# Reordering TensorE across units, spreading VectorE's other work over the weight steps, and a new DRAM layout for unit vectors and values

## The chip, the core and the metric

One core of one Trainium2 chip runs the whole program. The metric is the device time of one execution, in microseconds (us).

## The reference

The input `x` is [8, 32, 128, 128]. Two blocks follow each other, each on a group-normalized copy:

```python
x = x + wavelet_conv(gn(x), w0, w1, w2, bias)   # 3 Haar levels, a 5x5 conv of 128 channels on each
x = x + local_similarity(gn(x), spatial)
# local_similarity, K = 5:
dot    = einsum('bchw,bckhw->bkhw', x, patches)          # patches: the 25 shifted copies
sim    = dot / maximum(norm_x * norm_p, 1e-8)
weight = (sim + 1) * 0.5 * spatial_weight
out    = einsum('bckhw,bkhw->bchw', patches, weight)
```

## The kernel before

There are eight images. Iteration `i` of the main loop does the wavelet convolution of image `i` and the local similarity of image `b = i - 1`, interleaved. Iteration 0 has the convolution alone, iterations 1 to 7 have both, iteration 8 the similarity alone.

An iteration has a head and eight units. In the head the second normalization is found, the low-pass bands are made, levels 2 and 1 are convolved (L1232), and the unit vectors of units 0 and 1 are prepared. The level-0 convolution has eight points of 30 matmuls each (`conv_points`, L1258); each point is worked on together with one unit (half a band of the image) of the local similarity, so "unit j" is both.

What TensorE does beside the 30 matmuls is placed by `hook`, at the nine places `HOOKS`, k = 0 to 8. In each of the steps k = 0 to 7 `gram` (L1320) makes the products of keys and queries in one of two PSUM banks; `key_values` (L1303) turns the values around in two parts (before: k = 0 and k = 4), and `filter_group` (L1342) multiplies values by weights (before: k = 3, 5, 7 and 8). `norm_piece` (L1281) and `count_short` (L1291) prepare unit j + 2.

VectorE turns each product bank into weights (`weights`, L980), eight times in a unit. `gram` of step k waits until the weights of step k - 2 are made, and the weights of step k wait for `gram` of step k. Between the weights VectorE does all its other work by a list written out by hand in `iteration`: `units_open`, `units_refine`, `units_close`, `value_lows` and `unit_lows` (L948) of unit j + 2, `result` (L994) of unit j - 1, and the convolution's inputs and sums (`wino_in`, `wino_low`, `sums`, `accumulate`, `finals`, `add_up`, `image_stats`). The statistics of the next image (`raw_stats`, L741) stand in the head: four before `wino_delta`, two after the first unit vectors, two after `level1_out`.

Unit vectors and values go through DRAM. When `unit_lows` of unit h is done, the SyncE queue (SP) runs `save_half`: three transfers, `d_hl` (L374), `d_v` (L375) and `d_n` (L376). Then `load_unit` waits until all of them have landed, and issues 14 transfers: four for keys and four for queries (L390), two for values (L393), four for norms (L398). All of this is one queue in program order, with `load_residual` (L409) and `store_band` (L416) in it. Unit j of TensorE starts with `key_values`, which waits for the whole load of unit j (`unit_in`).

The GpSimd queue (POOL) loads the raw image into the four slots of `ring` (L454): chunks 0 to 3 for the statistics, chunks 4 to 7 as soon as `raw_stats` has read the slot, then chunks 0 to 3 a second time for the normalization, behind the store of `z1` (L508) and `load_up` (L488).

The three raw weight tensors are loaded at the start as 128 rows of 12,800 bytes each (L360), and then a matrix of 124 rows of 12,800 bytes, `tap_c` (L369).

Of the kernel before, what the change touches and what calls it, by code (L numbers as in the profile page):

```python
# [28 lines left out]
P = 128  # L29
C = 32  # L30
# [47 lines left out]
START = 1  # L78
POINT_MM = 3 * K
# [73 lines left out]
def build(nc, x, w0, w1, w2, bias, spatial, square, gather, tapmask, unpair, out):  # L153
    ctx = ExitStack()
    with ctx:
# [84 lines left out]
        d_hl = dram("d_hl", [B, 2 * BANDS, P, 2, FN], F16)  # L240
        d_v = dram("d_v", [B, 2 * BANDS, P, 2, FN], F16)
# [113 lines left out]
        def _(sp):  # L355
# [15 lines left out]
            def save_half(b, h):  # L371

                sp.wait_ge(unit_low, START + 8 * b + h + 1)
                sp.dma_start(d_hl[b, h], st_hl[:, :, h % 2, :]).then_inc(half_saved, 16)  # L374
                sp.dma_start(d_v[b, h], st_v[:, :, h % 2, :]).then_inc(half_saved, 16)  # L375
                sp.dma_start(d_n[b, h], st_n[0:P:C, h % 2, :]).then_inc(half_saved, 16)  # L376

            def load_unit(b, u):
                s = u % 2
                sp.wait_ge(half_saved, START + 48 * (8 * b + u + 1))  # L380
                alone(sp)

                if u >= 2:
                    sp.wait_ge(group_done, START + 4 * (8 * b + u - 1))
                else:
                    sp.wait_ge(group_done, START + 32 * b)

                for dst, order in ((keys[s], (0, 1, 0, 1)), (queries[s], (0, 0, 1, 1))):
                    for j, hl in enumerate(order):
                        sp.dma_start(dst[C * j:C * j + C].rearrange("c q e n -> c q (e n)"),  # L390
                                     d_hl[b, u, :, hl, :].rearrange("(q c) n -> c q n", c=C)).then_inc(unit_in[s], 16)
                for hl in range(2):
                    sp.dma_start(values[s][C * hl:C * hl + C].rearrange("c q e n -> c q (e n)"),  # L393
                                 d_v[b, u, :, hl, :].rearrange("(q c) n -> c q n", c=C)).then_inc(unit_in[s], 16)
# [48 lines left out]
        def _(pool):  # L443
# [88 lines left out]
            pool.wait_ge(half_saved, START + 8 * 48 * B)  # L532
# [3 lines left out]
        def _(act):  # L536
# [64 lines left out]
            def half_in(b, h):  # L601
# [9 lines left out]
                act.wait_ge(half_saved, START + 48 * (8 * b + h - 1 if h >= 2 else 8 * b))  # L611
# [11 lines left out]
            def norms(b, h):  # L623

                for p in range(2):
                    act.wait_ge(n2_ready, 16 * b + 2 * h + p + 1)

                    if p == 0:
                        act.wait_ge(unit_vec, START + 8 * b + h)
                    copy(st_a[:, p * PIECE:(p + 1) * PIECE], stat_ps[:, 0:PIECE], func=ACT.Abs_reciprocal_sqrt,  # L630
                         bias=tiny[:, :])
                    copy(st_n[:, h % 2, p * PIECE:(p + 1) * PIECE], stat_ps[:, 0:PIECE]).then_inc(n2_kept, 1)
# [5 lines left out]
            def vals_out(b, u, part):  # L638
                act.wait_ge(vt_ready, 16 * b + 2 * u + part + 1)
                act.wait_ge(group_done, START + 4 * (8 * b + u))  # L640
                copy(vals[:, 16 * part:16 * part + 16, :].rearrange("p n c -> p (n c)"), vals_ps[0:KN, :]).then_inc(vals_done, 1)

            def iteration(i, conv, ls):
# [18 lines left out]
                if ls:  # L662
                    norms(b, 0)
                    unit_highs(b, 0)
                    norms(b, 1)
# [10 lines left out]
                for j in range(CONV_TILES):  # L676
                    if ls:
                        vals_out(b, j, 0)
                    if conv and j == 1:
                        root(gn1, gn1_var, gn1_root, i + 1)  # L680
                    if conv and j + 1 < CONV_TILES:
                        wino_high(i, j + 1)
                    if ls and j + 2 < 2 * BANDS:
                        norms(b, j + 2)
                    if ls:
                        vals_out(b, j, 1)
                    if conv:
                        keep_point(i, j)
# [36 lines left out]
        def _(dve):  # L725
# [91 lines left out]
            def wino_in(i, p):  # L817

                half, kind = p // ROWS4, p % ROWS4
                dve.wait_ge(t_ready, 8 * i + p)  # L820
# [4 lines left out]
                if kind == 0:  # L825
                    wino_chain.link(dve, V.tensor_tensor(e2, two_rows(delta, 3), two_rows(delta, 1), ALU.subtract))
                    wino_chain.link(dve, stt(e2, two_rows(xa, H0 // 2 * half + 3), -2.25, e2))
                    V.tensor_tensor(point[0], even, odd, ALU.add)
                    V.tensor_tensor(point[1], even, odd, ALU.subtract).then_inc(t_wide, 1)  # L829
                elif kind == 1:  # L830
                    wino_chain.link(dve, V.tensor_tensor(t2, two_rows(delta, 4), two_rows(delta, 0), ALU.add))
                    stt(t2, two_rows(delta, 2), -4.25, t2).then_inc(t_wide, 1)
                elif kind == 2:
                    wino_chain.link(dve, stt(e2, two_rows(delta, 3), 4.0, two_rows(delta, 1), op1=ALU.subtract))
                    stt(point[0], odd, 2.0, even)
                    stt(point[1], odd, -2.0, even).then_inc(t_wide, 1)
                else:
                    wino_chain.link(dve, stt(e2, two_rows(delta, 1), -4.0, two_rows(delta, 3)))
                    stt(point[0], odd, 0.5, even)
                    stt(point[1], odd, -0.5, even).then_inc(t_wide, 1)  # L840
# [30 lines left out]
            def accumulate(n, p):  # L871
# [7 lines left out]
                for pair in range(2):  # L879
                    acc = two_rows(xa, 2 + H0 // 2 * half + 2 * pair)  # L880
                    if kind == 0:
                        stt(acc, acc, x_gain, s2).then_inc(acc_step, 1)
                    else:
# [616 lines left out]
```

## Time and profile before

| | us |
|---|---|
| median of 3 runs (2197.22 to 2202.63) | 2198.71 |
| the profiled execution, its own time | 2198.11 |
| span of its trace | 2196.5 |
| TensorE busy | 1666.1 (76%) |
| VectorE busy | 1506.4 (69%) |
| ScalarE busy | 629.4 (29%) |

1.6 us of the profiled execution lie outside its span.

Times in the rows are in us from the span's start unless ns is written. A row of the windows gives from:to, the length, the busy time and the number of instructions of PE, PEld (weight loads), DVE, ACT and POOL, the granted clock of TensorE as a share, the mean busy share of the 16 DMA engines, and GB/s. A row of the waits gives the engine and line that waited, what ended the wait, the total, the number of waits and the longest. A row of the timeline gives start, duration, engine, line, operation, output<-input, how many instructions were merged, and in brackets the idle time before and what ended it. SPq is SyncE's queue: its rows are the issues of transfers, not the transfers.

### The profile page before, as it was taken

The numbers are of one execution on the slowest core, as the hardware profiler recorded it, in microseconds if no ns is written. First come the engines' busy times: TensorE is split into PE (matmuls) and PEld (weight loads), VectorE is DVE, ScalarE is ACT, GpSimd is POOL, SyncE is SP. The second block draws the span as 40 slices with busy tenths as digits, with TensorE's granted clock in tenths as the row PEclk, the third lists the DMA queues.
The fourth block names the chain that finished last, engine by engine and source line by source line (L and its number), as shares of the span: only waits on it lengthen the run. The fifth ranks groups of instructions, "written<-read, shape, count | busy, mean of one in ns | idle before, by whom it ended". The sixth has DMA issues, their size and how long they took to land.

```text
span 2196.5 us, 49122 instructions
## 1 busy us (share of the span) xinstructions
PE 1666.1 (76%) x16895; PEld 883.3 (40%) x16895; DVE 1506.4 (69%) x2313; ACT 629.4 (29%) x1030; POOL 448.3 (20%) x791
## 2 busy tenths in 40 slices
PE   4777796787877797778877786778878787775575
PEld 3543353334433353334433353334433343332343
DVE  6427767876588567876588667885678666785564
ACT  2321232223332232323333232323223132322331
POOL 1352331014200232013300242012400242011000
PEclk8978997879878897788878897788978898777555
DMA  5252366564955567663956466564955567563775
GB/s 167 77 126 77 113 166 164 153 157 115 223 139 152 149 168 162 154 169 108 222 135 154 129 171 169 138 179 114 222 131 159 137 159 180 126 177 103 167 170 126
DMA packets 216642, 329.95 MB, mean 150 GB/s; under 512 B 51189, under 2 KB 182261, under 8 KB 215797
## 3 DMA queue, kind: packets, MB, share of 16 engines
q1 hardware_dynamic: 174832, 207.19, 38.4%
q0 software_dynamic: 41472, 118.24, 19.7%
q8 instruction: 214, 3.51, 0.7%
q14 instruction: 124, 1.01, 0.2%
HBM read 238.70 MB, written 86.61 MB: 148 GB/s over the span
## 4 chain that ended last, share of the span: by engine, by line
DVE 29%; PE 25%; issue 17%; SPq 13%; DMA 12%; DVEq 2%; ACT 2%; POOL 0%; POOLq 0%; ACTq 0%
PE conv L1258 7%; DMA unit_mem<-d_n 6%; DMA d_n<-st_n 5%; SPq L390 5%; DVE wgt L980 4%; PE conv L1232 4%; PE gram L1320 4%; SPq L398 4%; PE out_ps L1342 2%; PE vals_ps L1303 2%; DVE eo L795 2%; PE conv L1217 2%; DVE st_n L928 2%; DVE st_a L926 2%; PE conv L1441 2%
## 5 line engine op out<-in xcount | busy, mean ns | idle before, releaser
L1258 PE MATMUL conv<-thl,wconv 128*128 128x496 f16 (+2 forms) x1920 | 574.6, 431 | 20.8 <-DVE xa L855 8.3
L980 DVE SCALAR_TENSOR_TENSOR wgt<-gram,tapw 124x512 f32<-124x512 f32 x512 | 347.9, 688 | 349.2 <-PE gram L1320 316.5
L454 POOL DMA_DIRECT2D ring<-in_x x576 | 333.7, 584 | 322.3 <-ACT xa L538 222.4
L1320 PE MATMUL gram<-unit_mem 128*60 128x128 f16 x4096 | 267.6, 259 | 119.6 <-DVE wgt L980 114.7
L1342 PE MATMUL out_ps<-wgt,vals 124*32 124x128 f32 x4096 | 199.8, 323 | 122.5 <-DVE wgt L980 98.1
L1320 PEld LDWEIGHTS gram<-unit_mem 128*60 128x60 f16 x4096 | 164.3, 121 | 315.1 <-issue 309.0
L1258 PEld LDWEIGHTS conv<-thl,wconv 128*128 128x128 f16 x1920 | 174.2, 107 | 254.1 <-issue 120.5
L1232 PE MATMUL conv<-thl,wconv 128*128 128x480 f16 (+7 forms) x1200 | 251.7, 367 | 0.0
L538 ACT ACTIVATE vals<-vals_ps 124x512 f32<-124x512 f32 x128 | 76.2, 595 | 419.5 <-PE vals_ps L1303 419.5
L1342 PEld LDWEIGHTS out_ps<-wgt,vals 124*32 124x32 f32 x4096 | 115.2, 124 | 188.3 <-DVE wgt L980 124.1
L488 POOL DMA_DIRECT2D up<-d_z x128 | 68.6, 539 | 596.9 <-DVE xa L909 566.5
L538 ACT ACTIVATE st_hl<-st_b 128x720 f16<-128x720 f32 x64 | 52.7, 823 | 431.8 <-DVE st_b L937 431.8
L1303 PE MATMUL vals_ps<-unpair_c,unit_mem 64*60 64x32 f16 x4096 | 106.8, 194 | 79.2 <-DMA unit_mem<-d_n 70.3
L1232 PEld LDWEIGHTS conv<-thl,wconv 128*128 128x128 f16 x1200 | 116.2, 98 | 123.1 <-issue 4.5
L1303 PEld LDWEIGHTS vals_ps<-unpair_c,unit_mem 64*60 64x60 f16 x4096 | 95.3, 127 | 129.1 <-issue 129.0
L1281 PE MATMUL stat_ps<-st_n,sq_c 128*128 128x306 f32 x256 | 123.9, 573 | 30.5 <-issue 20.0
L538 ACT ACTIVATE st_a<-stat_ps,tiny 128x306 f32<-128x306 f32 x128 | 65.8, 514 | 202.5 <-PE stat_ps L1281 202.5
L1217 PE MATMUL conv<-xa,gat_c 128*128 128x512 f32 x128 | 74.3, 730 | 47.7 <-ACT xa L538 27.2
L475 POOL DMA_DIRECT2D d_x<-x x32 | 18.0, 565 | 406.2 <-DVE x L795 405.1
L538 ACT ACTIVATE thl<-tw 128x1024 f16<-128x1024 f32 x64 | 67.2, 1050 | 97.7 <-DVE tw L829 54.6
L845 DVE TENSOR_TENSOR thl<-tw,thl 128x1024 f16<-128x1024 f32 x64 | 78.0, 1219 | 9.6 <-ACT thl L538 9.6
L538 ACT ACTIVATE xa<-ring,gn 128x512 f32<-128x512 f32 x68 | 53.1, 837 | 91.5 <-DVE x L795 82.2
(132 smaller groups left out, 2007.2 us busy)
## 6 DMA issues: line engine op xcount, KB each, us to landing
unit_mem<-d_hl SPq DMA_DIRECT2D x512, 180.0 KB
ring<-in_x POOLq DMA_DIRECT2D x288, 128.0 KB, 3.4
ring<-in_x POOLq DMA_DIRECT2D x288, 127.0 KB, 3.5
d_hl<-st_hl SPq DMA_DIRECT2D x64, 360.0 KB
d_v<-st_v SPq DMA_DIRECT2D x64, 360.0 KB
unit_mem<-d_v SPq DMA_DIRECT2D x128, 180.0 KB
up<-d_z POOLq DMA_DIRECT2D x160, 128.0 KB, 2.8
d_x<-x POOLq DMA_DIRECT2D x32, 512.0 KB, 4.2
```

Of the source, the lines that this page charges most:

```text
L390: sp.dma_start(dst[C * j:C * j + C].rearrange("c q e n -> c q (e n)"), d_hl[b, u, :, hl, :].rearrange("(q c) n -> c q n", c=C)).then_inc(u ...
L398: sp.dma_start(norm_strips[s][row:row + 1, e % 2].rearrange("a (n w) -> a n w", w=KW), norms[:, :, TW * e:TW * e + KW]).then_inc(unit_in[s ...
L454: pool.dma_start(dst, src).then_inc(raw_in[slot], 16)
L538: return nc.scalar.activation(dst, src, func, bias=bias, scale=scale)
L980: V.scalar_tensor_tensor(out=dst, in0=g, scalar=SIM_SCALE ** 2, in1=tapw[:, :].unsqueeze(1).to_broadcast([KN, 2, 2 * QN]), op0=ALU.add, op ...
L1217: last = mm(dst, gat_c[:, q, :], src[:, 2 * r0 + q // 2:2 * r1:2, q % 2:2 * side:2], start=(q == 0), stop=(q == Q - 1))
L1232: last = mm(dst[:, a0 - r0:a1 - r0, b0:b1], wconv[:, level - 1, w, t, :], src[:, a0 + dy:a1 + dy, b0 + dx:b1 + dx], start=(n == 0), stop=( ...
L1258: last = mm(dst[:, :, b0:b1], wconv0[:, w, 2 * (p % ROWS4) + s, dx + 2, :], thl[:, p % 2, d, s, :, b0 + dx:b1 + dx] if p % ROWS4 != 1 else ...
L1281: mm(stat_ps[:, 0:PIECE], same_quadrant, st_n[:, h % 2, p * PIECE:(p + 1) * PIECE], start=True, stop=True)\
L1303: last = mm(vals_ps[row:row + KQ, C * n:C * n + C], values[s][0:2 * C, q, e, TH * KW * g:TH * KW * g + KQ], unpair_c[:, :], start=True, st ...
L1320: last = mm(bank[row:row + KQ, col:col + QN], key[:, q, e_at, TH * KW * g:TH * KW * g + KQ], tile[:, :, TH * g + 1:TH * g + 1 + TH, 1:1 + ...
L1342: last = mm(o[C * g:C * g + C, :, :, TW * e:TW * e + TW], vals[:, (e * BANDS + g) * 2 + c, :], wgt[:, e % 2, g, c * QN:(c + 1) * QN], star ...
```

## The change

The order of instructions on TensorE, VectorE and ScalarE changes, and so does the layout of two DRAM tensors. No arithmetic instruction is added or removed.

- **DRAM layout.** `d_hl` and `d_v` are [B, 8, 2, C, Q, FN], high part first and then the low part, with the four quadrants of a channel beside each other, instead of [B, 8, P, 2, FN]. A save of a unit is four transfers of 128 rows of 1,440 bytes, whose side in DRAM counts 4 x 32 x 720 elements, and the norms: five instead of three. A load has two transfers for the keys (64 rows of 5,760 bytes), four for the queries (32 rows) and one for the values (64 rows), and the four of the norms: 11 instead of 14. The bytes are the same.
- **Waits of the load.** A slot is free when the last products and the last turned values of its earlier unit are made, not when its last filter is done.
- **TensorE.** The products of step 0 come first in a unit. The last filter of unit j - 1 moves into step 1 of unit j; the two `key_values` move to steps 1 and 5, the filters to 4, 5, 7 and the next unit's 1, the norms to 0 and 2.
- **VectorE.** `value_lows` moves from step 2 to 0, `result` from 1 to 2, `wino_low` from 2 to 1; `wino_in`, `accumulate`, `finals` and `image_stats` are split over two or four steps; `wino_in` is at steps 6 and 7 instead of 5. All eight `raw_stats` leave their places in the head: two stand ahead of `level1_out`, two behind it, four in steps 0 to 3 of unit 0. The first normalization of the next image moves from unit 0 to units 1 and 2.
- **ScalarE.** `wino_high`, the norms, `vals_out` and `keep_point` are put in the order in which TensorE now makes their inputs.

```diff
-        d_hl = dram("d_hl", [B, 2 * BANDS, P, 2, FN], F16)
-        d_v = dram("d_v", [B, 2 * BANDS, P, 2, FN], F16)
+        d_hl = dram("d_hl", [B, 2 * BANDS, 2, C, Q, FN], F16)
+        d_v = dram("d_v", [B, 2 * BANDS, 2, C, Q, FN], F16)
...
-                sp.dma_start(d_hl[b, h], st_hl[:, :, h % 2, :]).then_inc(half_saved, 16)
-                sp.dma_start(d_v[b, h], st_v[:, :, h % 2, :]).then_inc(half_saved, 16)
+                for hl in range(2):
+                    sp.dma_start(d_hl[b, h, hl].rearrange("c q n -> q c n"), st_hl[:, hl, h % 2, :]).then_inc(half_saved, 16)
+                for hl in range(2):
+                    sp.dma_start(d_v[b, h, hl].rearrange("c q n -> q c n"), st_v[:, hl, h % 2, :]).then_inc(half_saved, 16)
...
                 if u >= 2:
-                    sp.wait_ge(group_done, START + 4 * (8 * b + u - 1))
+                    sp.wait_ge(gram_ready, 8 * (8 * b + u - 1))
+                    alone(sp)
+                    sp.wait_ge(vt_ready, 16 * b + 2 * (u - 1))
...
-                for dst, order in ((keys[s], (0, 1, 0, 1)), (queries[s], (0, 0, 1, 1))):
-                    for j, hl in enumerate(order):
-                        sp.dma_start(dst[C * j:C * j + C].rearrange("c q e n -> c q (e n)"),
-                                     d_hl[b, u, :, hl, :].rearrange("(q c) n -> c q n", c=C)).then_inc(unit_in[s], 16)
-                for hl in range(2):
-                    sp.dma_start(values[s][C * hl:C * hl + C].rearrange("c q e n -> c q (e n)"),
-                                 d_v[b, u, :, hl, :].rearrange("(q c) n -> c q n", c=C)).then_inc(unit_in[s], 16)
+                for j in range(2):
+                    sp.dma_start(keys[s][2 * C * j:2 * C * (j + 1)].rearrange("c q e n -> c (q e n)"),
+                                 d_hl[b, u].rearrange("l c q n -> (l c) (q n)")).then_inc(unit_in[s], 16)
+                for j, hl in enumerate((0, 0, 1, 1)):
+                    sp.dma_start(queries[s][C * j:C * j + C].rearrange("c q e n -> c (q e n)"),
+                                 d_hl[b, u, hl].rearrange("c q n -> c (q n)")).then_inc(unit_in[s], 16)
+                sp.dma_start(values[s][0:2 * C].rearrange("c q e n -> c (q e n)"),
+                             d_v[b, u].rearrange("l c q n -> (l c) (q n)")).then_inc(unit_in[s], 16)
...
                 if conv:
-                    for c in range(SLOTS):
-                        raw_stats(i + 1, c)
                     wino_delta(i, 0)
...
                 if conv:
+                    raw_stats(i + 1, 0)
+                    raw_stats(i + 1, 1)
                     level1_out(i, 0)
...
                     level1_out(i, 1)
-                    raw_stats(i + 1, SLOTS + 2)
-                    raw_stats(i + 1, SLOTS + 3)
-                    gn_open(gn1, bn1, bn1_done, gn1_part, i + 1, CHUNKS)
+                    raw_stats(i + 1, 2)
+                    raw_stats(i + 1, 3)
...
+                            if k < 4 and j == 0:
+                                raw_stats(i + 1, SLOTS + k)
...
-                            if k == 5 and j + 2 < CONV_TILES:
-                                wino_in(i, j + 2)
+                            if k in (6, 7) and j + 2 < CONV_TILES:
+                                wino_in(i, j + 2, k - 6)
...
-                                key_values(b, j, 0)
+                                unit_here(b, j)
                             if k == 4:
-                                key_values(b, j, 1)
+                                filter_group(b, j, 0)
                             if k < PAIRS:
                                 gram(b, j, k, short_ones[0])
-                            if k in (3, 5, 7, 8):
-                                filter_group(b, j, (k - 3) // 2 if k < 8 else 3)
+                            if k == 1:
+                                if j > 0:
+                                    filter_group(b, j - 1, 3)
+                                key_values(b, j, 0)
+                            if k == 5:
+                                filter_group(b, j, 1)
+                                key_values(b, j, 1)
+                            if k == 7:
+                                filter_group(b, j, 2)
```

## Rows read from the trace of the kernel before

**Rows 1.** Windows of iteration 4: head, unit 0, units 1 to 5, unit 6, unit 7.
```profile
1001.30:1065.04 63.74, 56.29 (x296) 31.40 (x285) 38.75 (x60) 19.87 (x35) 22.59 (x39) 0.92 0.60 159
1065.04:1091.73 26.69, 17.03 (x233) 8.82 (x233) 17.98 (x31) 8.45 (x13) 11.96 (x21) 0.87 0.97 225
1091.73:1216.95 125.22, 94.70 (x1140) 47.13 (x1141) 104.27 (x155) 38.18 (x62) 10.92 (x20) 0.79 0.56 142
1216.95:1235.38 18.43, 15.81 (x222) 7.94 (x223) 8.99 (x14) 3.12 (x5) 1.28 (x3) 0.87 0.71 182
1235.38:1253.81 18.43, 16.80 (x222) 8.14 (x222) 9.57 (x14) 4.79 (x7) 4.61 (x8) 0.82 0.39 109
```

**Rows 2.** Waits in units 1 to 5 of iteration 4, from 1091.73 to 1216.95.
```profile
DVE wgt L980 <- PE gram L1320: 21.9, 12, 7.7
...
PE gram L1320 <- DVE wgt L980: 14.5, 9, 3.3
PE out_ps L1342 <- DVE wgt L980: 13.4, 5, 3.2
```

**Rows 3.** Timeline of VectorE: first weights of unit 2, iteration 4.
```profile
1119.25 0.69 DVE L980 SCALAR_TENSOR_TENSOR wgt<-gram,tapw 124x512 f32<-124x512 f32 x1 [2.52 <-PE gram L1320]
```

**Rows 4.** Timeline of TensorE: starts of units 1 and 7, iteration 4.
```profile
1091.73 1.03 PE L1303 MATMUL vals_ps<-unpair_c,unit_mem 64*60 64x32 f16 x32 [4.67 <-DMA unit_mem<-d_n]
```
```profile
1235.38 1.03 PE L1303 MATMUL vals_ps<-unpair_c,unit_mem 64*60 64x32 f16 x32 [2.62 <-DMA unit_mem<-d_n]
```

**Rows 5.** Timeline of the SP queue: save and load of unit 3, iteration 4.
```profile
1116.84 0.64 SPq L374 DMA_DIRECT2D d_hl<-st_hl  x1
...
1120.99 4.59 SPq L390 DMA_DIRECT2D unit_mem<-d_hl  x8
...
1126.62 4.09 SPq L398 DMA_DIRECT2D unit_mem<-d_n  x4
```

**Rows 6.** Windows: weights loading, tap matrix, a save, a load, then a crowded stretch.
```profile
5.00:20.00 15.00, 9.86 (x40) 9.70 (x41) 7.19 (x4) 3.56 (x5) 6.49 (x12) 1.00 1.01 307
30.00:40.00 10.00, 3.12 (x7) 1.98 (x8) 8.63 (x13) 0.63 (x2) 0.00 (x0) 0.51 0.25 68
1118.20:1120.20 2.00, 2.00 (x14) 0.79 (x12) 0.95 (x2) 1.54 (x2) 0.00 (x0) 0.50 0.99 361
1149.50:1157.50 8.00, 8.00 (x116) 4.18 (x115) 7.54 (x10) 3.24 (x7) 0.00 (x0) 0.98 1.00 225
1055.00:1091.60 36.60, 27.07 (x284) 13.50 (x282) 19.00 (x34) 9.99 (x16) 11.96 (x21) 0.91 0.98 227
```

**Rows 7.** Timeline of the SP queue: head and unit 0 of iteration 4.
```profile
1044.95 0.67 SPq L374 DMA_DIRECT2D d_hl<-st_hl  x1
...
1050.70 3.73 SPq L390 DMA_DIRECT2D unit_mem<-d_hl  x8
...
1062.29 0.66 SPq L374 DMA_DIRECT2D d_hl<-st_hl  x1
```

**Rows 8.** Timeline of POOL: last ring loads for statistics, last for the normalization.
```profile
1048.64 2.42 POOL L454 DMA_DIRECT2D ring<-in_x  x4 [0.27 <-issue]
...
1080.77 2.30 POOL L454 DMA_DIRECT2D ring<-in_x  x4 [0.59 <-issue]
```

**Rows 9.** Timeline of VectorE: `units_open` of unit 0, iteration 4.
```profile
1037.98 0.80 DVE L920 TENSOR_TENSOR st_b<-st_a 128x612 f32<-128x612 f32 x1 [0.26 <-ACT st_n L538]
```

**Rows 10.** Windows: iteration 8, start of unit 0 to start of unit 7.
```profile
2048.86:2175.21 126.35, 88.33 (x1380) 59.45 (x1381) 78.02 (x132) 37.36 (x62) 0.00 (x0) 0.53 0.69 165
```

**Rows 11.** Timeline of the SP queue: saves of units 2 to 4, iteration 8.
```profile
2065.04 0.64 SPq L374 DMA_DIRECT2D d_hl<-st_hl  x1
...
2073.96 3.67 SPq L398 DMA_DIRECT2D unit_mem<-d_n  x4
2082.78 0.64 SPq L374 DMA_DIRECT2D d_hl<-st_hl  x1
...
2101.72 0.66 SPq L374 DMA_DIRECT2D d_hl<-st_hl  x1
```

More of the change, by code:

```diff
@@ L621, in half_in, with norms @@
                 copy(in_strips(st_v[:, 0, half, :]), strips(part)).then_inc(v_high, 1)
[L623 to L632, printed above, removed]
+            def norms(b, h, p):
+                act.wait_ge(n2_ready, 16 * b + 2 * h + p + 1)
+                if p == 0:
+                    act.wait_ge(unit_vec, START + 8 * b + h)
+                copy(st_a[:, p * PIECE:(p + 1) * PIECE], stat_ps[:, 0:PIECE], func=ACT.Abs_reciprocal_sqrt,
+                     bias=tiny[:, :])
+                copy(st_n[:, h % 2, p * PIECE:(p + 1) * PIECE], stat_ps[:, 0:PIECE]).then_inc(n2_kept, 1)
             def unit_highs(b, h):
@@ L639, in vals_out @@
                 act.wait_ge(vt_ready, 16 * b + 2 * u + part + 1)
-                act.wait_ge(group_done, START + 4 * (8 * b + u))
+                act.wait_ge(group_done, START + 4 * (8 * b + u) - (2 if u > 0 and part == 0 else 0))
                 copy(vals[:, 16 * part:16 * part + 16, :].rearrange("p n c -> p (n c)"), vals_ps[0:KN, :]).then_inc(vals_done, 1)
@@ new lines, in wino_in @@
+                if step != 0:
+                    if kind == 0:
+                        V.tensor_tensor(point[0], even, odd, ALU.add)
+                        V.tensor_tensor(point[1], even, odd, ALU.subtract).then_inc(t_wide, 1)
+                    elif kind == 1:
+                        stt(t2, two_rows(delta, 2), -4.25, t2).then_inc(t_wide, 1)
+                    else:
+                        far = 2.0 if kind == 2 else 0.5
+                        stt(point[0], odd, far, even)
+                        stt(point[1], odd, -far, even).then_inc(t_wide, 1)
@@ L869, in first_point, with accumulate @@
                 V.tensor_tensor(row, row, m, ALU.subtract).then_inc(acc_step, 1)
-            def accumulate(n, p):
+            def accumulate(n, p, pair):
                 kind, half = p % ROWS4, p // ROWS4
@@ L878, in accumulate, with finals @@
                     dve.wait_ge(live_kept, n + 1)
[L879 to L883, printed above, removed]
-                        stt(acc, s2, 1.0 if pair == 0 else 4.0, acc).then_inc(acc_step, 1)
-            def finals(n, half):
+                acc = two_rows(xa, 2 + H0 // 2 * half + 2 * pair)
+                if kind == 0:
+                    stt(acc, acc, x_gain, s2).then_inc(acc_step, 1)
+                else:
+                    stt(acc, s2, 1.0 if pair == 0 else 4.0, acc).then_inc(acc_step, 1)
+            def finals(n, half, pair):
                 dve.wait_ge(acc_step, acc_count(n, 4 * half, SUMS_AT[3]))
@@ L1013, in iteration @@
                     sums(b, 7)
-                    finals(b, 1)
+                    finals(b, 1, 0)
+                    finals(b, 1, 1)
                 set_live(i)
                 if ls:
-                    image_stats(b, 1)
+                    for t in range(4):
+                        image_stats(b, 1, t)
                     gn_open(gn2, bn2, bn2_done, gn2_part, b, 8)
@@ L1088, in iteration @@
                                 sums(i, j - 1)
-                            if k == 1 and j in (4,):
-                                finals(i, 0)
-                            if k == 1 and j in (1, 3, 5, 7):
-                                accumulate(i, j - 1)
-                            if k == 3 and j in (1, 2, 5, 6):
+                            if k in (1, 2) and j == 4:
+                                finals(i, 0, k - 1)
+                            if k in (1, 2) and j in (1, 3, 5, 7):
+                                accumulate(i, j - 1, k - 1)
```

113 lines of the change are left out of this document (56 added, 57 removed).

## The prediction

> **What bounds the kernel now.** I read the page first, and then windows, because an iteration has stages with different limits. The windows of iteration 4 [rows 1] cut it at the starts of units. The reader is to see four stages. In the head TensorE is busy for 56.3 of 63.7 us: it is the bound. In units 1 to 5 VectorE is busy for 104.3 of 125.2 us and TensorE for 94.7: neither is full, they wait for each other. In unit 0 the DMA engines are at a share of 0.97. In units 6 and 7 VectorE has little to do.
>
> The waits of units 1 to 5 [rows 2] show both directions: 21.9 us of VectorE's weights waiting for products, and 14.5 + 13.4 us of TensorE waiting for weights. That is a loop of two engines with uneven steps. A typical wait stands at the start of a unit, 2.52 us [rows 3]: TensorE does the last filter and `key_values` before the first products.
>
> The timeline of TensorE then shows that two units in each iteration start when their load lands: unit 1 waited 4.67 us and unit 7 2.62 us [rows 4]. So save plus load of a unit is on the path at those two places. The SP queue gives the chain [rows 5]: the save of unit 3 is issued at 1116.84, the first load at 1120.99 (4.15 us later), and the last norm is issued by 1130.71.
>
> **Part 1: TensorE's order and VectorE's even steps.** The work stays; what can go is VectorE's idle time. Of the 21.9 us [rows 2] the longest wait, 7.7 us, is almost all the wait for unit 1's load and is not the order's. That leaves 14.2 us in five units. The bounds are 0 (each wait comes back at another step) and 16 (a bit of the rest too). With the new order the first products of a unit come before filter and values, and each VectorE step carries about 104.3 / 40 = 2.6 us, against 94.7 / 40 = 2.4 us of TensorE. VectorE is then the longer engine at nearly each step, so most of the waits go, but not where an early step is short and TensorE has filter and values together (steps 1 and 5). I take 12 us of 14.2. Units 6 and 7 are governed by loads or by TensorE's own 16 to 17 us, so I put no gain there. The splits of `wino_in`, `accumulate`, `finals` and `image_stats` cost nothing: the instructions are the same.
>
> **Part 2: the save.** This is where I differ from a reading by bytes. A save moves 4 x 128 rows of 1,440 bytes, 737 KB. Before, it ran on all engines: 361 GB/s at a share of 0.99 [rows 6], so 2.0 us. Its side in DRAM now counts 4 quadrants first. What does the chip do with a transfer whose outer count has few divisors? The trace has one: the tap matrix, 124 = 4 x 31 rows, ran at a share of 0.25 and 68 GB/s, while a stretch with the weights in 128 rows of the same length ran at 1.01 and 307 GB/s [rows 6]. It used a quarter of the engines. An outer count of 4 can be dealt to four engines at most, if it is dealt by that count. Then the save goes at 361 / 4 = 90 GB/s and takes 8.2 us: 6.1 us more. At the tap matrix's 68 GB/s it would be 10.8 us, 8.8 more; if it is dealt over all 16, only the two more issues of 0.6 us are added, 1.3 us at most, and they overlap. I take +6.1.
>
> The Trainium skill (DMA: Bandwidth & Descriptors, "Why a DMA increments its semaphore by 16 and not by 1") states that a transfer uses the largest number of engines up to 16 that divides the outermost count of both sides. By that rule, the trace agrees: 124 gives 4 engines, a share of 0.25. The rule gives 4 engines for the new save too, and a time on the side of the 8.2 us.
>
> **Part 3: the load.** Three issues fewer. One takes 4.59 / 8 = 0.57 us at most and about 0.47 in [rows 7] (3.73 / 8): 1.4 us earlier. Do long rows move faster? The load of 1.84 MB went at 225 GB/s with a share of 1.00 [rows 6], so 8.2 us. 12,800-byte rows went at 307 GB/s, but to 128 partitions, where a load here goes to 32 or 64. At 307 the data would take 6.0 us; since the issues take about 7 us, little of that shows. I take 1.4 (bounds 0 and 2.2).
>
> Save and load together are +4.7 us from `unit_lows` to landing. In the quiet case that chain was 4.15 + 9.7 + about 3 for the last landing = 16.9 us, now 21.6. A unit will last (125.2 - 12) / 5 = 22.6 us and its load is started about one unit ahead. So units 2 to 6 are covered by 1 us, and where other transfers crowd in they are not: +1.5 us in an iteration (bounds 0 and 8). If part 1 gives more, this cover goes.
>
> Unit 7 has no cover: it waits for its load already [rows 4], and unit 6 is short (15.8 us of TensorE work in 18.4). +5.7 us there: 4.7 and 1 for four engines that share with ring loads.
>
> **Part 4: unit 0 and unit 1.** `unit_lows` of unit 0 does not come earlier when the statistics leave: `units_open` started 0.26 us after ScalarE's norm [rows 9], which follows TensorE's fixed place. The save at 1044.95 [rows 7] now ends near 1056.7 in place of 1050.5; the load of unit 0 (7 us of issues, 3 to land, 2 to 3 for the ring beside it) lands near 1069, where TensorE was ready for it at 1065.04 [rows 1]. The queue is in order: residual, save 1 (1062.29 before, near 1066 now), load 1. Meanwhile the ring loads of chunks 4 to 7, which were issued by 1051.1 [rows 8], wait for `raw_stats` and fall after 1056 and after 1066, and the four second loads end some 5 us later than 1083.1. That stretch was already at a share of 0.98 and 227 GB/s [rows 6]. Moving 2.1 MB into it is 9.2 us of all engines, and the save's slower rate comes on top; against that, part of the ring can fall behind the load of unit 1. I take +6 us for the start of unit 1 (bounds 0 and 10). The statistics and `gn_open` in unit 0 (about 3 us of VectorE) are covered by that wait; without it unit 0 has 18.0 us of VectorE in 26.7 anyway.
>
> **Iteration 8** has no convolution: from unit 0 to unit 7 126.4 us, VectorE 78.0 busy, TensorE 88.3 [rows 10]. The saves of units 2 and 4 lie 36.7 us apart [rows 11]; in that pair the queue stood idle between the end of load 2 (2077.6) and save 3 (2082.78), 5.2 us. +4.7 on each save-load pair less that slack is 2 x 4.7 - 5.2 = 4.2, and more where a save waits behind store and residual: I take 2.4 us for each of 7 units and 4 at the start, +20 us (bounds 0 and 33).
>
> **Sum.** An iteration: -12 + 1.5 + 5.7 + 6 = +1.2; seven of them +8. Iteration 8 +20. Iteration 0 has no local similarity: 0. Together +28 on the execution's own 2198.1 us, which is 0.6 below the median: 2226 us.
>
> **Rivals.**
> - *The save is dealt over all engines* (faster). For it: the SBUF side counts 128, and only the tap matrix speaks against. Then the save-load chain is unchanged, load 1 leaves before the second ring loads, and unit 1 starts about 5 us earlier. An iteration is -12 - 5 = -17, seven -119, iteration 8 0: 2079 us. It decides at a save of under 3 us of data. Chance 0.13.
> - *The slow save hides* (faster): four engines, but the ring gives way. Unit 1 +2, units 1 to 5 -14, unit 7 +4.7: -7.3, times 7 -51, iteration 8 +15: 2162 us. It decides where unit 1's start moves by less than 3 us. For it: the ring's shift takes competition out of 1045 to 1055. Against: the share of 0.98 behind it. Chance 0.18.
> - *The waits of the two engines only move*: 0 in place of -12, 13.2 us an iteration, 92 and 20: 2310 us. For it: TensorE has filter and values together at steps 1 and 5. Against: VectorE's sum is larger. Chance 0.07.
> - *The forecast*: chance 0.62, its own range 2185 to 2280.
>
> **Numbers.** A measurement of this kernel tells 0.3%, 6.6 us, from no change. Of the forecast's 0.62, 0.02 lies faster, 0.08 within, 0.52 slower; with the rivals faster 0.33, same 0.08, slower 0.59. The range 2150 to 2285 takes in the second rival and leaves out the first and the third, 0.20.
>
> **What would show it.** After the change the window of a save should have a DMA share near 0.25 and some 90 GB/s, and the time from the first `d_hl` issue to the first load issue should be about 10 us instead of 4.15. TensorE's wait for DMA at units 1 and 7 should grow to 6 to 9 us and about 8 us, and appear in iteration 8 at each unit. The weights' wait for products in units 1 to 5 should fall from 14 to about 2 to 4 us, and those five units should last about 115 us. If a save shows a share near 1, step 2 is wrong and the time is near 2080; if units 1 to 5 stay at 125, step 1 is.

## The result and the profile after

The changed kernel takes 2354.65 us (median of 4 runs, 2345.45 to 2357.0) against 2197.97 (median of 4, 2195.6 to 2202.63) before: ratio 1.0702, interval 1.0669 to 1.0736. It is slower, as forecast, but by 157 us and not by 28: 2226 was too low and the range, 2150 to 2285, does not hold it. Its profiled span is 2355.4 us.

First the page: its busy times, and its summary of the chain that ended last.

```profile
PE 1637.3 (70%) x16895; PEld 863.7 (37%) x16895; DVE 1505.9 (64%) x2313; ACT 639.1 (27%) x1030; POOL 448.3 (19%) x791
...
DMA 25%; PE 22%; SPq 20%; DVE 17%; issue 11%; ACT 2%; DVEq 1%; POOL 0%; ACTq 0%; POOLq 0%
```

VectorE is as busy as before in microseconds (1506) and TensorE a little less (1637 against 1666), while the span grew. So the new time is waiting, and 45% of the chain is transfers and the SP queue (25% before).

The windows of iteration 4 of the changed kernel are cut at the first products of a unit: head, unit 0, units 1 to 5, unit 6, unit 7, and then iteration 8 from unit 0 to unit 7.

```profile
1058.83:1130.22 71.39, 55.58 (x321) 30.54 (x320) 38.94 (x61) 21.05 (x36) 22.86 (x40) 0.94 0.48 123
1130.22:1163.78 33.56, 16.88 (x212) 8.50 (x212) 17.85 (x27) 8.66 (x13) 11.70 (x21) 0.75 0.82 205
1163.78:1288.34 124.56, 90.46 (x1144) 45.22 (x1145) 104.72 (x159) 38.71 (x62) 12.20 (x22) 0.83 0.60 149
1288.34:1310.95 22.61, 15.56 (x222) 7.72 (x222) 8.90 (x14) 2.28 (x4) 0.00 (x0) 0.88 0.61 156
1310.95:1329.50 18.55, 18.03 (x238) 8.81 (x238) 10.00 (x16) 4.88 (x7) 4.61 (x8) 0.78 0.30 83
2187.82:2338.25 150.43, 81.37 (x1365) 53.08 (x1365) 78.25 (x132) 37.47 (x62) 0.00 (x0) 0.59 0.57 142
```

Against [rows 1] and [rows 10] the busy times of VectorE and ScalarE are nearly the same in every stage. TensorE's are 4 to 7 us less in the two long ones, at a higher granted clock (0.83 against 0.79, and 0.59 against 0.53). The lengths of the stages went another way: unit 0 33.6 against 26.7, unit 6 22.6 against 18.4, iteration 8 150.4 against 126.4. Units 1 to 5 lasted 124.6 us, not the 115 that I expected. The cuts lie a little differently in the two kernels (before, a unit begins with the turning of values), so head and unit 7 are best taken together.

The waits of units 1 to 5 in the same iteration, to be laid beside [rows 2]:

```profile
PE gram L1333 <- DMA unit_mem<-d_n: 31.4, 4, 15.7
...
DVE wgt L991 <- PE gram L1333: 21.7, 9, 12.9
...
PE gram L1333 <- DVE wgt L991: 5.7, 5, 1.3
```

TensorE's waits for weights fell from 14.5 + 13.4 to 5.7 us. That loop of the two engines is gone. In its place TensorE waits four times for a load, 31.4 us, and VectorE waits behind it. The timeline of TensorE at the starts of units 0, 1, 3 and 7 shows it:

```profile
1130.22 0.64 PE L1333 MATMUL gram<-unit_mem 128*60 128x128 f16 x8 [8.27 <-DMA unit_mem<-d_n]
...
1163.78 0.42 PE L1333 MATMUL gram<-unit_mem 128*60 128x128 f16 x4 [15.72 <-DMA unit_mem<-d_n]
...
1213.81 0.42 PE L1333 MATMUL gram<-unit_mem 128*60 128x128 f16 x4 [5.58 <-DMA unit_mem<-d_n]
...
1310.95 0.64 PE L1333 MATMUL gram<-unit_mem 128*60 128x128 f16 x8 [6.93 <-DMA unit_mem<-d_n]
```

The queue of SyncE gives the reason. Its timeline for units 0 and 1 of iteration 4, and then a quiet save and load, unit 4's:

```profile
1101.79 1.48 SPq L376 DMA_DIRECT2D d_hl<-st_hl  x2
...
1123.57 1.49 SPq L376 DMA_DIRECT2D d_hl<-st_hl  x2
1125.15 6.41 SPq L378 DMA_DIRECT2D d_v<-st_v  x2
1131.77 3.59 SPq L379 DMA_DIRECT2D d_n<-st_n  x1
1144.40 1.24 SPq L394 DMA_DIRECT2D unit_mem<-d_hl  x2
...
1212.46 1.51 SPq L376 DMA_DIRECT2D d_hl<-st_hl  x2
1214.07 1.19 SPq L378 DMA_DIRECT2D d_v<-st_v  x2
1215.46 0.56 SPq L379 DMA_DIRECT2D d_n<-st_n  x1
1224.14 1.23 SPq L394 DMA_DIRECT2D unit_mem<-d_hl  x2
```

From the first issue of the quiet save to the first issue of its load are 1224.14 - 1212.46 = 11.7 us, where [rows 5] had 4.15. For unit 1 it is 1144.40 - 1123.57 = 20.8 us. There two issues of `d_v` took 6.41 us and one of `d_n` 3.59, against 1.19 and 0.56 in the quiet case: the issues themselves were held up.

Three windows of the changed kernel say what the engines did: in a quiet save (1215 to 1222), in its load (1226 to 1233), and in the slow save of unit 1 while ring loads run beside it.

```profile
1215.00:1222.00 7.00, 7.00 (x88) 3.37 (x86) 6.65 (x11) 4.33 (x7) 0.00 (x0) 0.87 0.27 94
...
1226.00:1233.00 7.00, 4.63 (x69) 2.11 (x61) 6.08 (x9) 2.68 (x4) 0.00 (x0) 1.00 1.00 240
...
1134.00:1143.50 9.50, 9.50 (x157) 5.23 (x153) 8.09 (x12) 2.62 (x5) 5.17 (x10) 0.95 0.63 209
```

The save runs at a share of 0.27 and 94 GB/s: four of sixteen engines, the figure that I had taken from the tap matrix [rows 6]. The load runs on all engines at 240 GB/s, where the old one had 225 [rows 6]. Over the whole run, the waits of the SP queue for landed saves:

```profile
SPq L350 <- DMA d_n<-st_n: 497.5, 64, 9.6
```

In the kernel before this wait (there L349) was 185.3 us, 64 times as well.

**Stage means.** One iteration is a small sample. The next table is worked out from the starts of the units' first products (before: of the first turned values) in iterations 2 to 6, the mean of five, in us. Unit 0 is from its start to that of unit 1; "last" is unit 7 with the next head.

```
                 unit 0  units 1-5  unit 6   last  iteration   iteration 8, units 0 to 6
before             27.3      125.1    18.0   79.4      249.8      126.3
after              33.8      124.9    23.5   86.7      268.8      150.4
difference         +6.5       -0.2    +5.5   +7.3      +19.0      +24.1
```

A wait at the start of a unit lengthens the unit before it: unit 7's wait for its load stands in the column of unit 6. I had predicted +6 for unit 0 and "last" together, -10.5 for units 1 to 5, +5.7 for unit 6, +1.2 for the iteration and +20 for iteration 8. Seven iterations of +19.0 are 133, with iteration 8 157 us: the whole difference.

### The profile page after: what moved, and what is told of

Same layout as the page of the kernel before. It is cut to its first block, busy times and chain, and to the rows that moved or that the text cites. A ratio compares the mean times of both kernels' runs of the same rounds, so it can differ in the third digit from the quotient of the medians.

```text
span 2355.4 us, 49229 instructions
## 1 busy us (share of the span) xinstructions
PE 1637.3 (70%) x16895; PEld 863.7 (37%) x16895; DVE 1505.9 (64%) x2313; ACT 639.1 (27%) x1030; POOL 448.3 (19%) x791
## 3 DMA queue, kind: packets, MB, share of 16 engines
q14 instruction: 130, 1.06, 0.2%
## 4 chain that ended last, share of the span: by engine, by line
DMA 25%; PE 22%; SPq 20%; DVE 17%; issue 11%; ACT 2%; DVEq 1%; POOL 0%; ACTq 0%; POOLq 0%
DMA d_n<-st_n 16%; DMA unit_mem<-d_n 9%; PE conv L1268 6%; SPq L404 5%; PE conv L1242 5%; SPq L378 5%; SPq L397 3%; PE gram L1333 3%; DVE wgt L991 2%; SPq L376 2%; SPq L394 2%; PE conv L1227 2%; PE out_ps L1355 2%; PE stat_ps L1291 2%; PE conv L1463 1%
## 5 line engine op out<-in xcount | busy, mean ns | idle before, releaser
L1268 PE MATMUL conv<-thl,wconv 128*128 128x496 f16 (+2 forms) x1920 | 565.4, 425 | 21.1 <-DVE xa L868 10.8
L1355 PE MATMUL out_ps<-wgt,vals 124*32 124x128 f32 x4096 | 191.2, 311 | 12.6 <-issue 7.4
L1291 PE MATMUL stat_ps<-st_n,sq_c 128*128 128x306 f32 x256 | 133.9, 615 | 18.8 <-issue 12.3
L1355 PEld LDWEIGHTS out_ps<-wgt,vals 124*32 124x32 f32 x4096 | 110.0, 121 | 68.4 <-issue 41.5
L1316 PE MATMUL vals_ps<-unpair_c,unit_mem 64*60 64x32 f16 x4096 | 96.4, 188 | 0.0
L1316 PEld LDWEIGHTS vals_ps<-unpair_c,unit_mem 64*60 64x60 f16 x4096 | 83.7, 118 | 32.1 <-issue 32.0
L544 ACT ACTIVATE x_res<-x_res,live,small 128x1024 f32<-128x1024 f32 x32 | 39.6, 1237 | 190.1 <-DMA x_res<-d_x 190.1
L544 ACT ACTIVATE sd<-conv 128x512 f32<-128x512 f32 x96 | 53.6, 593 | 116.2 <-PE conv L1268 57.5
```

Source lines behind the costliest of these rows:

```text
L544: return nc.scalar.activation(dst, src, func, bias=bias, scale=scale)
L1268: last = mm(dst[:, :, b0:b1], wconv0[:, w, 2 * (p % ROWS4) + s, dx + 2, :], thl[:, p % 2, d, s, :, b0 + dx:b1 + dx] if p % ROWS4 != 1 else ...
L1291: mm(stat_ps[:, 0:PIECE], same_quadrant, st_n[:, h % 2, p * PIECE:(p + 1) * PIECE], start=True, stop=True)\
L1316: last = mm(vals_ps[row:row + KQ, C * n:C * n + C], values[s][0:2 * C, q, e, TH * KW * g:TH * KW * g + KQ], unpair_c[:, :], start=True, st ...
L1355: last = mm(o[C * g:C * g + C, :, :, TW * e:TW * e + TW], vals[:, (e * BANDS + g) * 2 + c, :], wgt[:, e % 2, g, c * QN:(c + 1) * QN], star ...
```

## The experiments

Two theories stood against each other. **The save**: it runs on four engines because its DRAM side counts 4 first, and that alone makes the loss; the order by itself is a gain. **The order**: its waits only move, or it crowds the transfers, whatever the layout. Every ratio is to the kernel before, run on the same chip.

### The order without the layout, and the layout without the order

The first keeps everything of the change but the layout (3 saves, 14 load transfers, as before). The second is the kernel before with the new layout, saves and loads.

```diff
-        d_hl = dram("d_hl", [B, 2 * BANDS, 2, C, Q, FN], F16)
-        d_v = dram("d_v", [B, 2 * BANDS, 2, C, Q, FN], F16)
+        d_hl = dram("d_hl", [B, 2 * BANDS, P, 2, FN], F16)
+        d_v = dram("d_v", [B, 2 * BANDS, P, 2, FN], F16)
...
```

The saves and the loads go back with it. For the second kernel the same edit is made the other way, on the kernel before.

> The new order of TensorE, VectorE and ScalarE and the load's new waits, with the DRAM layout, the three saves and the fourteen transfers of a load as before. Theory A (the loss is the save on four engines): a save of unit 3 takes about 4 us to its landing as before, a middle unit 22 to 23 us instead of 25, unit 1 starts without a wait of more than 5 us; 12 to 19 us less in an iteration, 2065 to 2120 us. Theory B (the order itself costs what was lost, 22 us an iteration): 2300 us or more.

Measured: 2105.19 us (2095.41 to 2107.32), ratio 0.9586, interval 0.954 to 0.9632. Theory A's range holds it.

> The kernel before with the new layout of the unit vectors and values alone: five saves, eleven transfers of a load. Theory A: a quiet save takes 11 us instead of 4, and every unit waits for its load; an iteration is 17 to 27 us longer and iteration 8 some 24: 2340 to 2410 us. Theory B: near the kernel before, 2190 to 2230 us, since the loads have 6 to 12 us to spare in units 2 to 6.

Measured: 2329.17 us (2323.06 to 2332.15), ratio 1.0627, interval 1.0582 to 1.0671. That is 11 us below theory A's range and 99 above theory B's.

The change is thus a gain of 4% and a loss of 6%, put together. They don't add up: against the 2190.92 us of the kernel before on that chip they are -86 and +138, together +52, and the change cost 157. With the slow saves the order gives nothing: it even costs a little, 1.0702 against 1.0627.

Windows of the order alone, iteration 4, unit 0 and then units 1 to 5:

```profile
1031.59:1054.81 23.22, 18.53 (x214) 8.82 (x214) 16.98 (x26) 6.29 (x11) 9.41 (x17) 0.78 0.82 216
1054.81:1167.53 112.72, 88.82 (x1144) 44.50 (x1144) 104.14 (x159) 40.70 (x65) 14.84 (x27) 0.86 0.71 177
```

Waits of the order alone in units 1 to 5 of iteration 4:

```profile
PE gram L1330 <- DVE wgt L988: 6.9, 7, 1.2
...
PE gram L1330 <- DMA unit_mem<-d_n: 2.9, 2, 1.8
...
DVE wgt L988 <- PE gram L1330: 1.0, 2, 0.7
```

VectorE is busy for 104.1 of 112.7 us, and its wait for products is 1.0 us where it was 21.9 [rows 2]. TensorE's waits for weights are what they are in the changed kernel (6.9 and 5.7 us); the waits for loads differ, 2.9 against 31.4 us, and with them VectorE's wait behind them, 1.0 against 21.7. In the layout alone the SP queue waited 545.9 us for landed saves.

### The same saves, dealt to 16 and to 8 engines

These two kernels are the changed kernel with one edit: the four transfers of a save keep their 128 rows of 1,440 bytes, but their DRAM side counts 16 (or 8) first. Channels and quadrants land in another order in DRAM, so the data that the units load is permuted; instructions, rows and bytes are the same, and only the places of the rows in DRAM go with the count.

```diff
-  sp.dma_start(d_hl[b, h, hl].rearrange("c q n -> q c n"), ...)
+  sp.dma_start(d_hl[b, h, hl].rearrange("c q n -> (c q) n")
+                             .rearrange("(m k) n -> k m n", k=16), ...)   # and d_v; k=8 in the second
```

> The changed kernel with the same five saves, the same bytes and the same 128 rows of 1,440 bytes in each, but the rows are placed in DRAM in another order, so that the transfer's DRAM side counts 16 x 8 x 720 instead of 4 x 32 x 720. Channels and quadrants of unit vectors and values come back permuted, so this kernel computes other similarities; every instruction and every byte count is the same. Theory A (the outermost count deals the rows to engines): a save's DMA share is near 1 and it lands after 5 to 6 us; 2070 to 2130 us. Theory C (the save is slow because it is five transfers, or because its rows are scattered in DRAM): 2354 us as the changed kernel.

Measured: 2119.21 us (2115.62 to 2132.49), ratio 0.9684, interval 0.9632 to 0.9737. Time and landing (4.9 us) are theory A's; the share of 0.82 below is less than the "near 1" it named, and no run says why.

> As outer16 (channels and quadrants permuted in the same way), but the DRAM side of a save counts 8 x 16 x 720. Theory A (engines dealt by the outermost count): a save runs at about half of the DMA engines, 64 rows of 63 ns behind one another, and lands 6.3 to 7 us after its first issue (outer16: 4.9, the changed kernel: 11.0). The middle units of outer16 had 2 to 5 us to spare behind their loads, so most of the 1.5 to 2 us is covered: 2120 to 2155 us. Theory F (the time goes with the save's length in proportion, without cover: 2119 to 2355 us for 4.9 to 11.0 us): 2170 to 2190 us.

Measured: 2197.09 us (2188.65 to 2207.14), ratio 0.9998, interval 0.9973 to 1.0023.

A window inside a quiet save of each, first of the one with 16:

```profile
1088.60:1090.60 2.00, 2.00 (x11) 0.62 (x11) 1.80 (x3) 1.67 (x3) 0.00 (x0) 0.50 0.82 233
```

and of the one with 8:

```profile
1151.50:1155.50 4.00, 4.00 (x66) 1.90 (x66) 3.79 (x7) 1.88 (x4) 0.00 (x0) 0.80 0.52 168
```

Share and time go with the outermost count. Each save of unit 1 is that of iteration 4:

```
outermost count           4        8        16
share of DMA in a save    0.27     0.52     0.82
quiet save, us           11.0      7.0       4.9      (first issue to landing)
save of unit 1, us       20.7     13.7       8.9
waits of SP for saves   497.5    331.5     156.8
time, us               2354.65  2197.09   2119.21
```

The Trainium skill (DMA: Bandwidth & Descriptors, "Why a DMA increments its semaphore by 16 and not by 1") has the number of engines as the largest number up to 16 that divides the outermost counts of both sides. By that rule, the three runs agree: shares of 0.27 and 0.52 for 4 and 8, and above one half for 16.

My expectation for 8 was 2120 to 2155, and it missed; the rival's 2170 to 2190 missed too. The stages say why: units 1 to 5 took 114.3 us, all of the gain, but unit 0 took 29.9 and unit 7 with the head 81.8, where 16 engines gave 23.2 and 77.1. The slow saves of units 1 and 2 in the crowded stretch lose there 11 us an iteration. The middle has slack for 2 us more of save, the stretch of unit 0 has none.

### A save by quadrant

If the DRAM side counts 32 channels first, the same layout can be written without any permutation. The unit vectors and values share one tensor in SBUF and one in DRAM, and each transfer takes one quadrant of both.

```diff
-  for hl in range(2):
-      sp.dma_start(d_hl[b, h, hl].rearrange("c q n -> q c n"), st_hl[:, hl, h % 2, :])   # and d_v
+  for q in range(Q):
+      sp.dma_start(d_s[b, h, :, :, q, :].rearrange("l c n -> c l n"),
+                   st_s[C * q:C * q + C, :, h % 2, :])
```

> The changed kernel with unit vectors and values side by side in one SBUF and one DRAM tensor, saved as four transfers of one quadrant each (32 channels outermost, 4 rows of 1,440 bytes each), so again five transfers in all; the loads are the changed kernel's. Theory A: 32 deals to 16 engines, a save lands after 5 to 7 us (32 partitions at once may run at the 225 to 240 GB/s of the loads), 2070 to 2130 us. Theory C: 2354 us.

Measured: 2107.5 us (2105.62 to 2127.3), ratio 0.9636, interval 0.9572 to 0.97. A window in one of its quiet saves:

```profile
1081.80:1084.80 3.00, 3.00 (x29) 1.29 (x26) 2.10 (x4) 1.63 (x3) 0.00 (x0) 0.50 0.87 213
```

The full change in substance, with a quiet save of 4.9 us, is 4% faster than before, inside theory A's range. Its rows lie in DRAM just as those of the changed kernel do, and it also has five transfers; so neither the scattered rows nor the number of transfers (theory C) makes the slow save. It equals the order alone (2105.19), which has the old loads of short rows and a quiet save of 4.0 us. The loads themselves took as long in both: in iteration 4 11.2 to 15.1 us from first issue to landing, and 11.0 to 15.9. So the long rows and three fewer issues of the load gave nothing that can be seen.

### Which part of the order brings the gain

Both kernels have the old layout. The first has TensorE's and ScalarE's new order and the loads' new waits, with VectorE's lists as before. The second has VectorE's new lists (the moved statistics with them), ScalarE's new order and the loads' new waits too, with TensorE's order as before. The marks are against the changed kernel; the rest of both edits is left out.

```diff
 # TensorE's order alone: iteration() of VectorE as before
-                            if k < 4 and j == 0:
-                                raw_stats(i + 1, SLOTS + k)
...
-                            if k in (6, 7) and j + 2 < CONV_TILES:
-                                wino_in(i, j + 2, k - 6)
+                            if k == 5 and j + 2 < CONV_TILES:
+                                wino_in(i, j + 2)
 # VectorE's lists alone: iteration() of TensorE as before
-                            if k == 1:
-                                if j > 0:
-                                    filter_group(b, j - 1, 3)
-                                key_values(b, j, 0)
+                            if k in (3, 5, 7, 8):
+                                filter_group(b, j, (k - 3) // 2 if k < 8 else 3)
```

> Old layout, TensorE's and ScalarE's new order and the load's new waits, VectorE's lists as before (statistics too). Theory E1 (the wait at the start of a unit, 2.5 us, was TensorE's filter and values ahead of the first products): about 2 us less in each of units 1 to 5, 2120 to 2150 us. Theory E2 (the two orders only help together, since VectorE's long steps still hold the products): 2170 us or more.

Measured: 2206.51 us (2198.74 to 2214.26), ratio 1.0044, interval 1.0024 to 1.0064. This is theory E2's side.

> Old layout, VectorE's new lists and ScalarE's new order, TensorE's order as before. Theory E1: the wait at the start of a unit stays, the waits behind long steps go: 2150 to 2180 us. Theory E2: 2180 us or more.

Measured: 2125.92 us (2117.01 to 2140.53), ratio 0.967, interval 0.9641 to 0.97. It is faster than either theory said: the lists give most of the gain by themselves.

VectorE's waits for products over the whole run, one row from each kernel: TensorE's order alone,

```profile
DVE wgt L986 <- PE gram L1329: 318.1, 190, 8.3
```

VectorE's lists alone,

```profile
DVE wgt L988 <- PE gram L1327: 205.9, 142, 9.1
```

and both together with the old layout:

```profile
DVE wgt L988 <- PE gram L1330: 209.6, 149, 8.6
```

Before it was 316.5 us in 190 waits. TensorE's order leaves these waits as they were; VectorE's new lists take 111 us out of them. TensorE's order, worth nothing alone, adds some 18 us to the lists (0.967 to 0.9586; the intervals are 0.0009 apart), and units 1 to 5 go from 117.8 to 114.6. The lists were tried as a whole: that it is their evenness, and not another of their moves, is argued and not shown.

The granted clock rose as well, from 0.79 in units 1 to 5 of iteration 4 [rows 1] to 0.86. It doesn't carry the gain: in the kernel with VectorE's lists alone it lay between 0.81 and 0.86 in these units of iterations 2 to 6, and they took 117.6 to 118.1 us in each. In the changed kernel it was 0.83, and nothing was gained.

### The statistics put back

One edit on two kernels: all `raw_stats` return to their old places in the head, in the order alone and in the changed kernel.

```diff
+                    for c in range(SLOTS):
+                        raw_stats(i + 1, c)
                     wino_delta(i, 0)
...
-                            if k < 4 and j == 0:
-                                raw_stats(i + 1, SLOTS + k)
```

> The new order with the old layout (the run order_alone, 2105 us), but the eight statistics of the next image stand where the kernel before had them, so the ring loads of chunks 4 to 7 fall before unit 0 again. Theory A: the order's gain comes from units 1 to 5 (112.7 us there instead of 125.2) and the moved statistics matter little: 2095 to 2120 us. Theory D (the moved statistics brought unit 1's load ahead of the second ring loads and with it part of the gain, 3 to 5 us an iteration): 2125 to 2145 us.

Measured: 2135.83 us (2117.68 to 2137.63), ratio 0.9691, interval 0.966 to 0.9722. That is theory D's range.

> The changed kernel (2355 us) with the statistics where they were. Theory A1 (the ring loads moved into the crowded stretch are what makes save 1 take 21 us and unit 1 late): save 1 at 12 to 15 us, head and unit 0 some 5 to 8 us shorter in an iteration, 2300 to 2320 us. Theory A2 (the four engines alone do it, ring or no ring): within 15 us of 2355, as the run with the layout alone has saves of 15 us for units 0 and 1.

Measured: 2323.67 us (2322.82 to 2327.73), ratio 1.0578, interval 1.0556 to 1.06. It lies 4 us above theory A1's range and far below theory A2's.

The sign depends on the save. These pairs ran on different chips, so their ratios are compared. With fast saves the late statistics gain 1.05%, some 23 us (unit 0 22.9 us against 28.0, units 1 to 5 114.6 against 111.6); with slow saves they cost 1.24%, some 27 (unit 0 33.8 against 28.3, save of unit 1 20.7 us against 17.2; against that, the save of unit 0 took 11.1 and not 15.1). So of the 4% that the order gains, about a quarter is the moved statistics', and none of that is in units 1 to 5. The timeline of POOL in the changed kernel shows where the ring loads of the later chunks go:

```profile
1113.51 2.42 POOL L460 DMA_DIRECT2D ring<-in_x  x4 [17.16 <-DVE bn L750]
1127.39 2.42 POOL L460 DMA_DIRECT2D ring<-in_x  x4 [0.27 <-issue]
```

The first waited 17.16 us for a moved `raw_stats`, and the second starts inside the save of unit 1 (1123.57 to 1144).

## Why the prediction was wrong

**Part 1, the order: right.** I took -12 us for units 1 to 5. With the old layout they took 114.6 against 125.1 us, -10.5 in the mean and 112.7 against 125.2 in iteration 4. That it goes from the waits of the weights for products was right too: they fell to 1.0 us. Which half brings it I had not separated: it is VectorE's new lists. What I had at nothing is an effect of the order elsewhere. By itself it made unit 0 4.4 us and "last" 1.9 us shorter, and unit 6 4.1 us longer.

**Part 2, the save: the mechanism right, one term left out.** Four engines, a share of 0.27, 87 to 98 GB/s. I took +6.1; from 3.95 us the quiet save went to 10.9 to 11.7, that is +7.0 to +7.7, and more in crowded places (unit 2 from 7.2 to 18.3, unit 1 from 5.0 to 20.7). The sweep takes it apart. From 16 engines to 4 the quiet save goes from 4.9 to 11.0 us, +6.1: the engines cost just what I said, some 0.063 us for each row that one engine has to move in the save's four transfers. The other 1.0 us is there on 16 engines already (4.9 against 3.9 before): it came with the two more transfers, whose issues I had let overlap and put at nothing.

**Part 3, the load: wrong, and this is what made the rest go.** I took 1.4 us off for three issues. The issues did shorten, in iteration 4 from 8.8 to 11.0 us a load to 7.5 to 8.5. But the loads of its units 2 to 7 took 11.6 to 15.6 us from first issue to landing, 11.3 to 14.9 before: nothing came off. The load waits for data and not for issues: a window in it shows a share of 1.00 and 240 GB/s, as against 225 before [rows 6], with 5,760-byte rows taking nearly four times as long as 1,440-byte rows (a median of 392 and 104 ns in these windows). Part 3's own numbers said so, 8.2 us of data against 7 of issues. (The 307 GB/s that it holds beside them is of a window in which the GpSimd queue moved 17% of the bytes.) So the chain from `unit_lows` to landing grew by 8.4 us (17.0 to 25.4, mean of units 3 to 6 in iterations 2 to 6) and not by 4.7: 1.4 of the rest is the save's, 2.2 the load's.

**The failed step: "units 2 to 6 are covered by 1 us ... +1.5 us in an iteration".** The cover was the small difference of two large terms, 22.6 of unit against 21.6 of chain. With nearly 4 us more on the chain the sign turned, 22.6 against 25.4: units 3 to 6 wait 4 to 7 us each for their load, and the five units last 25.0 each in the mean, near the chain. The 10.5 us of part 1 were there (the waits of the engines on each other are gone) and were waited away at the loads. Units 1 to 5: predicted -10.5, measured -0.2. Seven times 10.3 is 72 us of the miss. My own bound for this step, 8 us in an iteration, would have given about 2270.

**Part 4, unit 0 and unit 1: right in place, less than half the size.** Predicted +6 in an iteration, measured 6.5 + 7.3 = +13.8: seven times 7.8 is 55 us of the miss. I priced the moved ring loads, and a quiet save behind them. With the statistics put back, +9.6 of the +13.8 stays: the moved ring loads are 4.2 of it, and the larger part is the slow save. In the crowded stretch it is slower again, by about the same factor on 16, 8 and 4 engines: 4.9 to 8.9, 7.0 to 13.7, 11.0 to 20.7 us, 1.8 to 2.0 times. So the slow save pays 9.7 us for this company where a fast one pays 4.0, and I had put 1 us for company, at unit 7 alone. And unit 0 itself waited 8.27 us for its load, in the head, where I had +4.

**Iteration 8: right, and by its mechanism.** +20 predicted, +24.1 measured. The chain grew there by 6.1 us a unit (17.3 to 23.4, units 0 to 5) instead of 4.7. With my slack of 5.2 us in a pair that makes 7.0 a pair, 24.5 us in seven units, without the 4 that I had added at the start.

**Unit 6: the number right, in part by luck.** +5.7 predicted, +5.5 measured. But the chain of unit 7 grew by 8.8 us (18.2 to 27.0), and its save was issued 4.3 us before unit 6 began instead of 0.4, since unit 6 itself had waited for its load. And the order alone, with fast saves, made unit 6 4.1 us longer: there the save of unit 7 was issued 2.1 us after unit 6's start and took 7.2 us instead of 5.8. For the order I had put nothing there.

**The rivals.** That the save is dealt over all engines is refuted for this kernel. Its price, -119 us, was too high for what such a save gives: the changed kernel with 16 engines ran 2119 and by quadrant 2107, 3.2 and 3.6% less than before, 70 to 80 us. Its -12 in units 1 to 5 and -5 about unit 1 came (-9.8 and -6.4 with 16 engines), but unit 6 took 4.7 us more. That the waits only move is refuted by the order alone; its 2310 us was the nearest of the four forecasts, by a path that did not happen. That the slow save hides is refuted by the start of unit 1, which waited 15.72 us for its load against 4.67 [rows 4].

**What is open.** That it is the ring loads which double the save of unit 1 was not tried by itself. They run beside it in the timeline, and putting their statistics back shortens it from 20.7 to 17.2 us. The traces as they are point the same way. With 16 engines all saves beside which the GpSimd queue moved nothing took 4.8 to 5.9 us, and all others 7.3 to 9.9; with 8 engines 6.9 to 8.6 and 8.9 to 17.1. In iteration 8, which loads no image, unit 1's save took 11.1, 8.0 and 5.1 us on 4, 8 and 16 engines. That queue also has loads and stores other than the ring's, so the ring is not singled out. The held-up issues are not what doubles the save: with the statistics back it took 17.2 us though its two `d_v` issues took 1.42 us, and on 8 engines 13.7 us with 1.31.

Two kernels beat both of the given ones: the order with the old layout, 2105.19 us, and the full change with saves by quadrant, 2107.5 us; their intervals overlap.

## What to carry to other kernels

Before changing a layout, write down the outermost count of both sides of each transfer: here a view that put a count of 4 ahead took three quarters of the DMA engines away, with the bytes and rows unchanged. A transfer's lengthening is judged by the chain that it stands in, and that chain against the stage's length after the speed-up, not before: a cover of 1 us that is the difference of two terms of 22 us is no cover. And try the parts of a change singly: a gain of 4% and a loss of 6% lay in this one diff, and the larger hid the smaller.

## What the runs showed of the hardware

- A DRAM-to-SBUF load into 32 or 64 partitions moved 225 GB/s in 1,440-byte rows [rows 6] and 240 GB/s in rows of 5,760 bytes, both at a share of 1.00. Rows four times as long gained 7% in rate and nothing in time.
- A save of 737 KB in four transfers, whose DRAM side counted 4, 8 or 16 first, had a DMA share of 0.27, 0.52 or 0.82 and landed in the quiet after 11.0, 7.0 or 4.9 us.
- Unit 1's save, beside other traffic, took nearly twice its quiet time on 16 engines (4.9 and 8.9 us), on 8 (7.0 and 13.7) and on 4 (11.0 and 20.7): on few engines the same factor costs more microseconds.
- Issues can be held up when a transfer is on few engines: on 4, two issues of unit 1's save in iteration 4 took 6.41 us, 1.19 in the quiet. On 8 and 16 engines the same two took 1.31 and 1.23 us in the same crowded place.
